# A transformer layer on one core: a wait of one PSUM copy taken out, and the batch loop written out

## What is computed

```python
h = _layernorm(x) * (1 + ca) + sa
x = x + ga * attention(h)        # 16 heads of 64
h = _layernorm(x) * (1 + cb) + sb
x = x + gb * ffn(h)              # gated MLP + top-k of product keys into 512 experts

# attention, per batch and head
sim  = q @ k.T * SCALE           # 256 x 256, causal mask
attn = softmax(sim)
out  = attn @ v                  # then gates, heads joined, @ Wout
```

## Time and profile before

| | |
|---|---|
| median of 2 runs | 1392.72 us (1392.15 to 1393.29) |
| the profiled execution, whole | 1396.35 us |
| its span, first to last instruction | 1394.6 us |
| granted TensorE clock, mean | 0.995 |
| PE busy | 1345.9 us, 97% of the span |
| ACT, DVE, POOL busy | 1256.3 (90%), 1227.5 (88%), 1087.0 us (78%) |

### The profile page before, as it was taken

The page is one execution under the profiler, slowest core; times in us unless marked ns, Lnnn a source line. Parts: engine busy times, 40 slices in busy tenths (PEclk is TensorE's granted clock), DMA queues, the critical chain, the costliest instruction groups (busy, mean ns, idle before and its releaser), DMA issues. The chain is left out here.

```text
span 1394.6 us, 39816 instructions
## 1 busy us (share of the span) xinstructions
PE 1345.9 (97%) x11491; PEld 1164.5 (84%) x11491; DVE 1227.5 (88%) x5314; ACT 1256.3 (90%) x4084; POOL 1087.0 (78%) x1252
## 2 busy tenths in 40 slices
PE   6889999999999999999999999999999999999998
PEld 4678888888888888888888888888888888888878
DVE  6678999888999888999888999988999988899977
ACT  6779999999999999999999999999999999999975
POOL 2138888888888888888888888888888888888770
PEclk9999999999999999999999999999999999999999
DMA  5000000000000000000000000000000000001000
GB/s 137 16 19 15 11 19 21 21 21 17 10 14 21 21 21 19 14 9 21 21 21 21 13 8 21 21 21 21 13 8 21 21 21 21 13 8 27 12 11 11
DMA packets 55649, 27.74 MB, mean 20 GB/s; under 512 B 10848, under 2 KB 54816, under 8 KB 55616
## 3 DMA queue, kind: packets, MB, share of 16 engines
q1 hardware_dynamic: 55376, 26.92, 7.4%
q10 hardware_dynamic: 240, 0.43, 0.1%
HBM read 23.02 MB, written 4.31 MB: 20 GB/s over the span
## 5 line engine op out<-in xcount | busy, mean ns | idle before, releaser
L696 ACT ACTIVATE pS<-pS,nmx 128x128 f32<-128x128 f32 (+1 forms) x1024 | 389.2, 435 | 38.3 <-DVE nmx L1121 38.2
L1121 DVE CUSTOM_DVE_ANT_0 pS<-pS,mask 128x128 f32<-128x128 f32 (+1 forms) x1024 | 331.3, 390 | 48.4 <-PE pS L1633 45.7
L528 POOL TENSOR_TENSOR fexp<-fexp,fsum 128x512 f32<-128x512 f32 x240 | 311.8, 1328 | 52.4 <-DVE fexp L1272 52.4
L519 POOL TENSOR_TENSOR fsum<-ex 128x512 f32<-128x512 f32 x248 | 252.0, 1046 | 0.0
L688 ACT COPY pT<-pS 128x768 f32<-128x768 f32 x256 | 200.8, 857 | 32.1 <-PE pW L1662 27.4
L1643 PE MATMUL pS<-ident,p_sb 128*128 128x128 f32 x1536 | 208.7, 276 | 5.7 <-DVE p_sb L1146 4.7
L1146 DVE TENSOR_TENSOR p_sb<-pS,coef 128x256 f32<-128x256 f32 (+2 forms) x512 | 206.3, 448 | 4.6
L696 ACT ACTIVATION_READ_ACCUMULATOR pS<-pS,nmx 128x1 f32 x1024 | 196.2, 192 | 0.0
L1643 PEld LDWEIGHTS pS<-ident,p_sb 128*128 128x128 f32 x1536 | 173.9, 142 | 19.3 <-DVE p_sb L1146 13.7
L676 ACT COPY qk<-pW 128x512 f32<-128x512 f32 x256 | 156.8, 612 | 18.7 <-PE pW L1577 15.0
L1658 PE MATMUL pW<-pT,v 128*64 128x256 f32 x1024 | 160.6, 392 | 0.4 <-ACT pT L688 0.4
(11 more groups left out here) (211 smaller groups left out, 3699.3 us busy)
## 6 DMA issues: line engine op xcount, KB each, us to landing
x_in<-in_L_attn_tokens SPq DMA_DIRECT2D x32, 128.0 KB, 2.1
x_res<-in_L_attn_tokens SPq DMA_DIRECT2D x32, 128.0 KB, 2.8
modA<-mods_dram SPq DMA_DIRECT2D x31, 128.0 KB, 3.1
out<-yo SPq DMA_DIRECT2D x31, 128.0 KB, 1.9
modG<-mods_dram SPq DMA_DIRECT2D x32, 64.0 KB, 2.9
modB<-mods_dram SPq DMA_DIRECT2D x32, 64.0 KB, 2.8
modC<-mods_dram SPq DMA_DIRECT2D x32, 64.0 KB, 3.0
fsum<-in_L_attn_Wkv SPq DMA_DIRECT2D x1, 512.0 KB, 6.4
```

Of the source, the lines that this page charges most:

```text
L519: ins = nc.gpsimd.tensor_tensor(fsum[:, k, h], ex[:, k, h, 0:NX].unsqueeze(2).broadcast_to([P, NX, NK]), ex[:, k, RH + h, :].unsqueeze(1). ...
L528: ins = nc.gpsimd.tensor_tensor(fexp[:, k, h, :], fexp[:, k, h, :], fsum[:, k, h].rearrange("p i j -> p (i j)"), ALU.mult)
L696: ins = nc.scalar.activation(ps, ps, ACT.Exp, bias=nmx[:, p % 2, h, k:k + 1], scale=-1.0, accum_out=den(p)[:, h, k:k + 1])
L1121: ins = nc.vector.tensor_tensor_reduce(out=ps, in0=ps, in1=mask[:, (1 - k) * P:2 * P], scale=-1.0, scalar=LARGEST, op0=ALU.add, op1=ALU.mi ...
```

## The change

The semaphore `pT0_read` is removed: `copy_transposes(2)` on ACT no longer waits for it, and the last matmul of `weigh_values(0)` on PE no longer increments it. The helper `run` calls `body(i)` with a plain number for each turn from -1 to 32, so that no engine has a loop; the waits compare with constants, and the DMA addresses are constants.

```diff
@@ -217,7 +217,6 @@
         p1_ready = ev("p1_ready", len(SHARED))
         t_full, pT_ready = ev("t_full", NP), ev("pT_ready", NP)
         coef_ready = ev("coef_ready", NP)
-        pT0_read = ev("pT0_read", 1)
         xT_high, h2T_high, h2T_mod = ev("xT_high", 1), ev("h2T_high", 1), ev("h2T_mod", 1)
@@ -391,11 +390,7 @@
         def run(eng, body, first=3, tail=1):
-            for i in range(-1, first):
-                body(i)
-            with eng.Fori(first, B - tail) as i:
-                body(i)
-            for i in range(B - tail, B + 1):
+            for i in range(-1, B + 1):
                 body(i)
@@ -683,8 +678,6 @@
                         act.wait_ge(S(t_full), at(t_full, b, p + 1))
-                        if p == 2:
-                            act.wait_ge(S(pT0_read), at(pT0_read, b, 1))
                         nc.scalar.copy(pT[:, p % 4], pS[:, p % 2, :, 0:SW]).then_inc(S(pT_ready), 1)
@@ -1663,8 +1656,6 @@
                         if p % 2 == 1:
                             w.filled(ins, "PV", p // 2)
-                        elif p == 0:
-                            ins.then_inc(S(pT0_read), 1)
```

## The result

The changed kernel took 1376.01 us (1375.62 to 1376.39) against 1392.72 for the kernel before: ratio 0.988, interval 0.9837 to 0.9922. Timed again in more rounds it took 1376.77 against 1396.22, ratio 0.9858 (0.9843 to 0.9874). The two runs of before that were given first lie lower than every later one (1393.67 to 1399.37), so the second figure is the better one: 19.5 us, where 20.2 were forecast. The two profiled executions, 1396.35 and 1375.62, are 20.7 apart.

The account below looks back on a forecast made before the run. PE was taken as the bound, busy 40.98 of a 41.60 us turn. 31 x (0.69 - 0.04) = 20.2 us saved, the loop at nothing, from 1392.72 gave 1372.5 us; range 1370 to 1376, 8 in 10 from 1368 to 1385.

Parts of the forecast that it names:

- The stall is PE's, and goes whole: At `scores(4)`, PE's wait for ACT's copy of pair 2 vanishes, saving 0.69 us a turn.
- What is late next: Four chains on other engines (second copy, DVE, POOL, DMA) checked after `scores(4)`; only POOL was charged, 0.04 a turn.
- The copy: ACT's copy of pair 2 starts 0.87 us sooner and ends 0.18 before PE reaches `scores(4)`.
- DVE is just in time: `row_max(4)` comes 0.65 us sooner; DVE falls 0.04 behind PE, which fits the room before PE's transposes.
- POOL's way: POOL's product for `transpose_experts(1)`, 0.30 us of room, moves by 0.40 to 0.50; PE loses nothing to 0.12 a turn.
- the 0.04: Loss a turn at `transpose_experts(1)`, where PE waits for POOL, taken from nothing to 0.12 us.
- The loop at nothing: Writing out the 28 looped turns costs or gains nothing, with 1.4 us allowed either way.
- (a): PE waits for POOL at `transpose_experts(1)`, up to 0.52 a turn; 5.3 to 13.3 us saved, about 1383; chance 0.13.
- (b): ACT's copy waits just as long for something else; nothing won, 1392.7 us; chance 0.03.
- (c): Instruction packets come late in straight code, stalling PE 1.04 us 28 times; 1402 us; chance 0.04.
- (d): Each loop pass costs a fetch or drained queue, which goes; 20.2 + 29 us saved, 1343.5 us; chance 0.03.

Follow-up runs that it names:

- `loop_nowait`: The kernel before with its loop kept and only the wait taken out: 1373.40 us, ratio 0.9843; measured again 1375.41 us, ratio 0.9855.
- `later_wait`: The changed kernel with the copy of pair 2 made to wait for `transpose_h`, 0.37 us later than the old wait: 1410.33 us, ratio 1.0095.

## Why the prediction was right

*The time.* The 1372.5 us forecast were 3.5 too low, because the two runs that it started from lay 3.5 below the later median of before; the saving, 20.2, was 0.7 too high.

*The stall is PE's, and goes whole.* Right: 0.69 a turn were worked out, `scores(4)` comes 0.70 sooner, and `loop_nowait` and `later_wait` show that a turn follows the wait one for one. The step that mattered was to take the 0.07 by which a matmul starts before the modelled end of the one ahead, over the 0.62 of printed idle time.

*What is late next.* The copy had more room than worked out: it starts 0.99 sooner, not 0.87, since ACT's next operation begins before the end printed for `rows2`. DVE is just in time, as forecast. POOL's way was rightly named as the tight one, and 0.10 to 0.14 are left of its 0.30, a hand-over included; the 0.04 charged to it did not come due. The pair of kernels with the delayed operation shows that its room is all but used up.

*The loop at nothing.* This term was mis-sized: 1.4 us either way were allowed, and the written-out form costs 0.13 a turn with the wait kept, 3.4 us (1.0024, interval clear of 1), and 0.06 with the wait out, some 2 us. I had compared one window, 41.65 against 41.60, and called the two equal. Of the cost, 0.7 us are the two long turns. In the usual turns 0.03 to 0.04 shows at `transpose_scores(0)`, which comes that much later against the border of the turn in both written-out kernels than in their looped ones; with the wait kept a further 0.05 shows at `scores(4)`. The errors cancelled: the wait alone is worth 31 x 0.67 = 20.8, more than the 20.2, and the form takes some of it back.

*Rivals.* (a), that POOL takes the stall over, did not happen, by some 0.05 us. (b) fell by the trace. (c) has at most a grain: the two long turns, 0.7 us, hang on DVE's instruction stream, not on PE's, and no late packet shows there; (c) needed 29. (d) fell: without the loop and with the wait the kernel is slower, not faster. Nor does the Trainium skill's reason to prefer full unrolling, the fetch that a taken branch can force (Runtime: NRT & Kernel Launch, Instruction fetch mechanics), show on this kernel: the two looped kernels, before and `loop_nowait`, show none and one instruction packet between 200 and 1260 us, and the branch back costs PE nothing that shows. The loop's border does show on DVE, where it is covered: in the loop `row_max(0)` follows the operation ahead of it by 0.09, and written out by 0.45, 0.44 of it a wait for PE. DVE comes there some 0.36 later in the loop, and that is hidden because the scores are ready only then.

By its turns the fastest version is the one with the wait out and the loop kept: 40.93 against 40.99 us, in two executions of each (27 turns take 1105.08 and 1105.19 against 1106.80 and 1107.13). Its whole time was 1373.40 against 1376.77 us on one chip, within the noise told of above.

## What to carry to other kernels

Where one engine is busy for nearly the whole of a turn and the waits name a single stall of it, a wait behind that stall can be worth its full length, as it was here, and it is worth asking of each wait whether the order of another engine already guards the buffer. Before summing, list the chains that run from before the removed stall to after it: each needs room of the stall's length, unless the change moves it too, as it moved POOL's, and those that have less are the next bound. And cost the two halves of a change apart: here the second gave back a part of what the first won.

## What was not expected

A looped turn was faster than a written-out one, by 0.06 us with the wait out and 0.13 with it kept, though the loop needs more instructions of the sequencers: the window shows no time on PE for them. What the written-out stream has instead is, by the likeliest reading, a place every 128 instructions on DVE where some 0.37 us comes on the path, if `row_max(0)` stands just there; the rest of the difference has no cause shown. And most of the scatter between runs of one kernel, up to 5 us, lies outside the middle turns in the two kernels where two traces can be set side by side: their 27 turns take 1105.08 and 1105.19 us in two executions of `loop_nowait` whose spans are 1371.3 and 1374.1, and 1106.80 and 1107.13 in two of the changed kernel with 1373.8 and 1377.3.
